# Narrow products for gathered groups, and a sixth sheet in layer 2 of a graph network

## What is computed

```python
def _hconv(x, src, dst, ew, w1, b1, w2, b2, g, b):
    h = jax.nn.relu(x @ w1 + b1)
    msg = ew[:, None] * h[src]
    agg = jax.ops.segment_sum(msg, dst, num_segments=x.shape[0])
    h = agg @ w2 + b2
    return jax.nn.relu(_bn(h, g, b))

x = x + gnn(layernorm(x), edges)      # two _hconv, each followed by a batch norm
x = x + ffn(layernorm(x))             # 8 experts of three products, weighted by a softmax gate
```

## Time and profile before

| | us |
|---|---|
| median of 3 runs | 4848.3 |
| span of the profiled execution | 5228.2 |
| TensorE busy | 4623.3 (88%) |
| VectorE busy | 2688.7 (51%) |
| ScalarE busy | 2435.6 (47%) |
| GpSimd busy | 2110.6 (40%) |
| gathers (line 1054), 2070 | 1989.1 busy |
| products of gathered groups (line 1138), 8280 matmuls | 111 ns between starts |
| products of sheets (line 1106), 3528 matmuls seen | 1251.9 busy |

### The profile page before, as it was taken

One profiled execution on the slowest core, in us unless ns is written; L12 is line 12 of the kernel. 1 busy time (PEld: TensorE's weight loads), 2 busy tenths in 40 slices (PEclk: granted clock), 3 DMA queues, 4 the chain that ended last, 5 costly groups with the idle time before them and its releaser, 6 DMA issues. The chain is left out here.

```text
span 5228.2 us, 71544 instructions
## 1 busy us (share of the span) xinstructions
PE 4623.3 (88%) x25508; PEld 3800.6 (73%) x25508; DVE 2688.7 (51%) x6606; ACT 2435.6 (47%) x4218; POOL 2110.6 (40%) x2284
## 2 busy tenths in 40 slices
PE   6778888888999579888988988649999999999999
PEld 5667777666677467776666666548888888888888
DVE  7666666566333464522222222366666666666665
ACT  4655556666211263300000000057777777777777
POOL 1466666566666456666666666630000000000000
PEclk9889999999999789999999999779999999999999
DMA  5467777566755247876666666431111111001110
GB/s 155 148 210 271 243 240 245 188 211 217 236 198 201 77 141 268 277 243 218 218 219 205 226 212 224 131 96 25 30 28 33 33 33 33 24 26 33 33 28 15
DMA packets 546618, 770.23 MB, mean 147 GB/s; under 512 B 149720, under 2 KB 441411, under 8 KB 546262
## 3 DMA queue, kind: packets, MB, share of 16 engines
q1 hardware_dynamic: 328176, 382.01, 21.7%
q0 software_dynamic: 100944, 273.96, 16.4%
q10 hardware_dynamic: 117142, 109.65, 6.5%
HBM read 605.58 MB, written 147.26 MB: 144 GB/s over the span
## 5 line engine op out<-in xcount | busy, mean ns | idle before, releaser
L1106 PE MATMUL pf<-work 128*128 128x330 f32 (+4 forms) x3528 | 1251.9, 491 | 63.3 <-DMA work<-front 31.3
L1054 POOL DMA_INDIRECT wst<-h,src_col x1040 | 1000.3, 962 | 541.9 <-issue 275.0
L1106 PEld LDWEIGHTS pf<-work 128*128 128x128 f32 x3528 | 661.0, 197 | 402.2 <-issue 220.1
L2096 DVE TENSOR_TENSOR f_hl<-f_hf,f_hh 128x1024 fp32r<-128x1024 f32 (+1 forms) x400 | 479.7, 1199 | 636.3 <-ACT f_hf L1959 636.0
L1952 ACT ACTIVATE f_hh<-f_p,f_sh,f_sc 128x512 fp32r<-128x512 f32 (+1 forms) x800 | 571.7, 768 | 395.9 <-PE f_p L2194 394.5
L1273 ACT ACTIVATE ah<-agg 128x1024 fp32r<-128x1024 f32 (+1 forms) x50 | 51.8, 1037 | 1464.2 <-DVE agg L1420 1086.6
L1138 PEld LDWEIGHTS ps<-oh,wst 128*128 128x128 f32 x4160 | 543.4, 203 | 144.5 <-issue 99.6
L1138 PE MATMUL ps<-oh,wst 128*128 128x128 f32 x4160 | 560.7, 288 | 88.6 <-issue 55.1
L1054 POOL DMA_INDIRECT f_xr<-h,src_col x518 | 497.7, 961 | 282.8 <-issue 134.0
L1054 POOL DMA_INDIRECT f_u<-h,src_col x512 | 491.1, 959 | 260.5 <-issue 136.7
L1959 ACT ACTIVATE f_hf<-f_p,f_sh,f_sc 128x512 f32<-128x512 f32 (+1 forms) x800 | 572.5, 775 | 0.0
(11 more groups left out here) (285 smaller groups left out, 7648.0 us busy)
## 6 DMA issues: line engine op xcount, KB each, us to landing
work<-h SPq DMA_DIRECT2D x216, 512.0 KB
work<-front SPq DMA_DIRECT2D x50, 924.0 KB
front<-agg ACTq DMA_DIRECT2D x12, 3300.0 KB
work<-front SPq DMA_DIRECT2D x50, 756.0 KB
work<-front SPq DMA_DIRECT2D x50, 660.0 KB
work<-front SPq DMA_DIRECT2D x50, 580.0 KB
front<-agg ACTq DMA_DIRECT2D x8, 2600.0 KB
work<-front SPq DMA_DIRECT2D x25, 832.0 KB
```

Source lines behind the costliest of these rows:

```text
L1054: g.indirect_dma_start(G[t % R], None, h_dram[layer], bass.IndirectOffsetOnAxis(ap=src_col[:, col:col + 1], axis=0)).then_inc(ga[t % R], 16)
L1106: ins = g.matmul(pF[:, k, 0:count * w].rearrange("p (s c) -> p s c", c=w), HB[a % 2][0:r, n, k * P:(k + 1) * P], x, start=b == 0, stop=b = ...
L2096: g.tensor_tensor(hlo[l][q % 2][:, :, 0:nn], hf[l][:, :, 0:nn], hhi[l][q % 2][:, :, 0:nn].bitcast(fp32), ALU.subtract).then_inc(f_lo[l], 1)
```

## The change

- Sheet 5 is added: 8 segments of 2 groups, width 56 (448 columns), windows of 9 nodes. It covers groups 140 to 155, is made in layer 2 after sheet 4, and is used in layer 2. Layer 2 gathers 235 groups (939 tiles). `HOT_Q` of layer 2 goes from 48 to 96, so tiles are made at the same rate for twice as long, and `ZERO_Q` from 53 to 101.
- The products of gathered groups (line 1138) move `width` columns of the matrix and write as many columns of PSUM.
- The planner's `other` counts 16 x max(64, 8 + width x 5 // 6) for a group's products, which was 16 x 111; the blocks are dealt out with that. In layer 2 up to four blocks stand behind a group, which was mostly two or three.
- The scratch of descriptors that GpSimd's DMAs use takes 8192 bytes of each SBUF partition, which was 16384.

```diff
-              (52, [(2, 2, 7), (6, 2, 8)])]
+              (52, [(2, 2, 7), (6, 2, 8)]),
+              (56, [(8, 2, 9)])]
-    MADE = [[3, 2, 1, 0], [4]]
-    USED = [[3, 2, 1, 0], [3, 2, 1, 0, 4]]
+    MADE = [[3, 2, 1, 0], [4, 5]]
+    USED = [[3, 2, 1, 0], [3, 2, 1, 0, 4, 5]]
...
-    HOT_Q = [188, 48]
+    HOT_Q = [188, 96]
...
-            other = [16 * 111 + sum(max(224, NB * hot(layer, t)[4] * 9 // 10) for t in hot_behind(layer, q))
+            other = [16 * max(64, 8 + width(FGL[layer] + q) * 5 // 6) + sum(max(224, NB * hot(layer, t)[4] * 9 // 10) for t in hot_behind(layer, q))
...
+                            wide = width(FGL[layer] + q)
                             for k in range(KC):
                                 for t in tiles_of[q]:
                                     if k == 0:
                                         g.wait_ge(ga[t % R], gathered_value(layer, t))
-                                    ins = g.matmul(pS[bank_of[q]][:, k, :], G[t % R][:, k * P:(k + 1) * P], OH[t % RO],
+                                    ins = g.matmul(pS[bank_of[q]][:, k, 0:wide], G[t % R][:, k * P:(k + 1) * P], OH[t % RO][:, 0:wide],
                                                    start=t == tiles_of[q][0], stop=t == tiles_of[q][-1])
...
-    nc = bacc.Bacc("TRN2", target_bir_lowering=False, num_devices=1)
+    nc = bacc.Bacc("TRN2", target_bir_lowering=False, num_devices=1, dynamic_dma_scratch_size=8192)
```

## The result

The changed kernel takes 5043.93 us (median of 4 runs, 5037.9 to 5049.81) where the kernel before takes 4850.36: ratio 1.040, 95% interval 1.039 to 1.042. It is 194 us slower; 105 us faster had been forecast.

A forecast was written before the change was run, and what follows sets the result against it. Gathers on GpSimd were taken as the bound, with waits for TensorE that less work there could win back. Layer 1 gives 90 us, layer 2 15: 4848 - 105 = 4743, say 4745 us, range 4650 to 4840.

The forecast's parts named there:

- 64 ns for an instruction: Gathered groups' products on TensorE: 64 ns each up to 68 columns, 5 + 0.83 per column above, between bounds 62 and 111.
- rival 1: Loading 128 x 128 weights binds at 107 to 111 ns, narrow products save nothing, layer 2 middle +100; 4950 us, chance 0.06.
- the 197 and 201 us "saved": TensorE time narrow products would save: layer 1 groups from 478 to 281 us, layer 2 from 449 to 248.
- The prediction's own sum: Layer 2, larger of TensorE's work and GpSimd's 5.01 us a group: 1268 before, 1234 after, 34 us less.
- The step on the 380 us: Profile exceeds median by 380 us; half taken from gather waits, leaving 290 us: 161 in layer 1, 129 in layer 2.
- The first end: All 380 us lie in the 480 us of gather waits, leaving 100 us of waits in an ordinary run.
- rival 2: All 380 us are the profiler's, ordinary waits are 100 us; layer 1 gives 39, layer 2 15; 4794 us, chance 0.17.
- the reading of "remote": GpSimd's 370.5 us of gather idles put down to "remote" were taken as waits for TensorE's products, seen late.
- The 20 us for full queues: Layer 2, groups 0 to 62: DMA needs 5.7 us a group against TensorE's 5.4, costing 20 us more.
- The scratch at 0: Halving GpSimd's descriptor scratch to 8192 bytes was taken to cost 0 us.
- The block prices: Sheet blocks on TensorE: 375 ns per instruction of 448 columns, 147 us added in layer 2 by the new sheet.
- the gathers' own 1.252 us: GpSimd's gathers without waits start 1.252 us apart: 1336 us for layer 1, 1256 us for layer 2.

The follow-up runs named there:

- z1: The kernel before with narrow products whose weights are loaded in two halves of 64 columns, TensorE held up in that set; ratio 1.0157 to before.
- y1: The kernel before, unchanged, profiled again in a set where TensorE is held up; median 5219 us, span 5221 us.
- c2: The kernel before plus the sixth sheet and small scratch, full width, old planner price, TensorE running freely; 5014.69 us beside 4848.34, ratio 1.0345.
- a1: The changed kernel with the gathered products' weights loaded in two halves of 64 columns, TensorE running freely; 5009.41 us, ratio 1.0341 to before.
- c1: The changed kernel with all but sheet 5's first and last blocks cut to 56 of 448 columns, TensorE running freely; 5020.13 us, ratio 1.0350 to before.
- x3: The changed kernel with the planner's old price of 16 x 111 for a group's products, TensorE held up; 5310 us, ratio 1.0111 to before.
- x1: The kernel before with narrow products alone, in a set where TensorE is held up; ratio 1.0031 to before.
- b4: The kernel before with narrow products alone, measured a second time where TensorE is held up; ratio 1.0039 to before.
- a2: The changed kernel with each load of sheet 5 bringing an eighth of its sheet data, TensorE running freely; 5043.74 us, ratio 1.0406 to before.

## Why the prediction was wrong

**The narrow products: the term that was mis-sized, and with it the sum.** The step put 64 ns for an instruction, from the 65 ns of 12 rows, between bounds of 62 and 111. It is 108 to 111 ns: the upper bound, rival 1. Of the 197 and 201 us "saved", 1.78 - 1.73 us a group or some 13 and 12 us are left. The error was to take the row with the nearest number of moving columns and not the one with the nearest weights. What sets the distance goes with the weights: 58 and 128 moving columns are equally far apart, and z1, with 64 columns of weights and the same moving columns, is at 45 ns. In rows 7 the loads have 12 and 40 rows of weights; that the rows matter is the likely reason why they are quicker, but no run here varied the rows alone. The Trainium skill, "TensorE: Matmul & The Clock Gate", section LDWEIGHTS, gives 107 ns for 128 columns, and the measured distance agrees; where it says that rows do not matter, rows 7 still speak against it. I had that rule before me, priced it as rival 1 and gave it 0.06; its middle, 4950 us, was still 94 us too low.

**What hangs on it.** With 111 ns TensorE's work in layer 2 is 1176 - 29 + 203 = 1350 us, not 1174. The instructions counted in the traces of y1 and c2, at the prices of the rows, give 1185 and 1360, so the 174 us added were rightly summed. That c2 lost nearly as much, 166 us, is no proof of it, since work and time need not go together. The prediction's own sum, the larger of TensorE's work and GpSimd's 5.01 us in blocks of 20 groups, gives 1271 us for the groups of y1 and 1390 for those of c2: 119 more, an estimate by this method with the right price. The other 47 us are not singled out; in its layer 2 c2 has 40 us of TensorE waiting on "work<-front" and a granted clock of 0.98. Rival 1 also named the mechanism and its price, 0 to 200 us in layer 2; the result is 186 there (1477.5 against 1291) and 19 in layer 1, which rival 1 left at zero.

**The base it was added to.** The step on the 380 us offered two ends and took the middle, 290 us of waits left. The first end was nearly right in place: 369 of the 380 lay in the gather stages (1603 to 1412 us and 1469 to 1291, the last worked out), and of waits 76 and 35 us were left, 111 in all. The cause was neither the profiler, as rival 2 had it, nor TensorE's work, as the reading of "remote" had it, but a condition of the set of runs. Less work on TensorE could not win those waits back. In a free set layer 2 of before was within 35 us of what its gathers need. TensorE had 115 us less work than the stage was long, but not where the sheet's work was put. By the same count the last 31 groups had 3.2 to 3.7 us of work each and the first 220 had 4.5 to 5.4 (means of 20 groups), beside GpSimd's 5.01. In c2 the first 220 groups have 5.1 to 6.5. So TensorE became the bound of most of layer 2: busy 95%, 1405 of 1477.5 us in the changed kernel, while GpSimd waits 345 us for it there. The 16 groups of gathers taken away shortened what was no longer the bound. That TensorE is the bound is read from these shares and waits; where its work was taken away again (a1, c1) only a part came through, in c1 with the clock as the reason.

**The clock.** The forecast left it out. Between c2 and the changed kernel it is 0.96 and 0.92 in layer 1, 0.98 and 0.95 in layer 2, with 19 and 20 us more there (28 between the medians and their sets). The difference holds the new price too. x3 gives the price no part that can be told, and with the width alone x1 and b4 lost clock and 15 and 23 us in held sets, so the clock is the likely cause; no run in a free set had the width alone.

**DMA and scratch.** The 20 us for full queues in groups 0 to 62 were not singled out: gathers 100 to 200 of layer 2 are the slowest, and TensorE waits on "work<-front" for 38 us of the whole layer, so some of it may be there. a2 cleared the last sheet's loads, not those. The scratch at 0 was right.

**What held.** The block prices (380 ns for 448 columns, 375 forecast), the gathers' own 1.252 us, VectorE's and ScalarE's work hidden, the experts at 1826 us.

**No version beats before.** Of all edits that keep the result only the half loads made TensorE cheaper. On before alone they met held sets both times, 1.2 to 1.6% slower. Whether they gain where TensorE is free stays open; a1's layer 1, 1416 us against 1412, promises little.

## What to carry to other kernels

Price a small product by its weight load as well as by its moving columns, and look for a row with the same weights; if none exists, the cautious bound is the value to take when the whole change rests on it. Before work is moved from one engine to another, take the bound from an execution of the same length as the timed runs: here a trace 8% longer than the median showed the receiving engine as the one that held everything, when in the timed runs the other was the bound. Then ask where the slack lies: 115 us of it over the stage took up little of the added work, since it lay in other groups. And a busy TensorE is not a fast one: in c1 the shorter products were run at a lower granted clock, which took back most of what they saved.

## What the runs showed of the hardware

- A float32 product with 128 x 128 weights starts 108 to 111 ns after the one before whether it moves 58 columns or 128 (the changed kernel, x1), and 215 ns after it at the lower level of the clock (c1). With 64 columns of weights, written to one half of the output's partitions and then to the other, it is 45 ns (z1). The first agrees with the section LDWEIGHTS of the Trainium skill's "TensorE: Matmul & The Clock Gate"; the last is below the 53 ns that its rule of columns / 1.2 gives for 64 columns.
- The granted clock was 0.63 over 100 us in which TensorE was busy 97%, with weight loads 94% of the time and 56 to 74 moving columns in nearly all products (c1); it was 0.97 over the same stretch with 448 columns in the blocks. The products turned slow after idles of 1.4 to 3.9 us and fast again during products of 512 columns.
- The semaphore of a product can move some microseconds late, again and again, while gathers and loads run, on the same chip in one set of runs and not in another. For before this costs 365 to 405 us (8%), 369 of the 380 us of its first profile in the two gather stages; the experts take 1830 us beside 1826. Its cause is open. The sign in a trace is idles of others put down to "remote", and gaps in TensorE's own row of products that wait for nothing.
